# Ternarizing the next weight slices ahead of a chunk's recurrence chain instead of behind it, with the slices' loads cut in four

## The reference, cut to what matters

```python
# xn: 2048 x 1024 per sequence, x_q: xn rounded to 8 bits per row
# W_q: weights rounded to -1, 0, 1 by the mean of |W|
dt = clip(softplus(bitlinear(xn, W_dt, b_dt)), 0.001, 1.0)
x_proj = bitlinear(xn, W_x, b_x)              # 2048 columns: b_t and c_t
b_t = clip(x_proj[..., :D], -5, 5)
c_t = clip(x_proj[..., D:], -5, 5)
alpha = exp(clip(dt * A, -10, 0))
prefix = cumprod(alpha)                       # along the 2048 positions
h = prefix * cumsum(dt * b_t / prefix_shift)
s = nan_to_num(h * tanh(c_t))
x = x + s * silu(xn @ W_ternary.T)
```

## Time and profile before

| quantity | value |
|---|---|
| time, median of 2 runs | 2427.0 us (2418.78 to 2435.22) |
| the profiled execution's own time | 2431.09 us |
| its span, slowest core (core 7) | 2429.5 us |
| spans of the 8 cores | 2399.9 to 2429.5 us |
| DVE busy over the span | 1376.0 us (57%) |
| PE busy over the span | 1017.7 us (42%) |
| ACT busy over the span | 694.0 us (29%) |

### The profile page before, as it was taken

The page is one execution under the profiler, slowest core; times in us unless marked ns, Lnnn a source line. Parts: engine busy times, 40 slices in busy tenths (PEclk is TensorE's granted clock), DMA queues, the critical chain, the costliest instruction groups (busy, mean ns, idle before and its releaser), DMA issues.

```text
span 2429.5 us, 17568 instructions; the slowest of 8 cores (2399.9 to 2429.5 us)
## 1 busy us (share of the span) xinstructions
PE 1017.7 (42%) x3686; PEld 373.7 (15%) x3686; DVE 1376.0 (57%) x1730; ACT 694.0 (29%) x877; POOL 27.8 (1%) x52
## 2 busy tenths in 40 slices
PE   0321142227999999970010310413362352352351
PEld 0000000002333333320000000201120120121120
DVE  1135566654443444432222377477878878878877
ACT  0543320026555555421108300000131131131130
POOL 0000000000000000000000000000000000000000
PEclk9999999558988999985555755555785686686685
DMA  2867500013232333202223000000011011011000
GB/s 41 240 175 226 171 1 0 0 45 124 83 104 70 104 105 100 100 19 86 85 95 123 1 0 0 26 0 3 6 52 45 7 52 52 0 52 52 0 35 35
DMA packets 63375, 153.18 MB, mean 63 GB/s; under 512 B 18003, under 2 KB 18132, under 8 KB 61205
## 3 DMA queue, kind: packets, MB, share of 16 engines
q1 hardware_dynamic: 58406, 126.89, 17.4%
q0 software_dynamic: 4864, 25.17, 2.7%
HBM read 135.25 MB, written 16.78 MB: 63 GB/s over the span
## 4 chain that ended last, share of the span: by engine, by line
DVE 35%; PE 28%; DMA 11%; ACT 10%; issue 8%; DVEq 5%; ACTq 1%; SPq 0%; PEldq 0%; PEld 0%; POOLq 0%; POOL 0%
PE psB L784 9%; PE psA L767 8%; PE psA L1017 5%; DMA x1spill<-poolf 5%; DVE poolf L374 4%; DVEq L110 4%; DMA poolf<-w2t 3%; ACT poolb L584 2%; ACT poolf L556 2%; ACT poolb L512 2%; DVE poolf L673 2%; PE psB L1091 2%; DMA poolf<-w1t 2%; ACT poolf L559 2%; ACT poolb L776 1%
## 5 line engine op out<-in xcount | busy, mean ns | idle before, releaser
L784 PE MATMUL psB<-poolb 128*128 128x512 bf16 x1024 | 265.1, 396 | 37.1 <-ACTq L110 29.5
L797 DVE TENSOR_TENSOR poolb<-psB,poolb 128x512 bf16<-128x512 f32 x224 | 155.0, 692 | 199.8 <-PE psB L784 199.2
L767 PE MATMUL psA<-poolb 128*128 128x512 bf16 x1024 | 244.7, 399 | 12.9 <-DVEq L110 12.9
L1091 PE MATMUL psB<-poolb 128*128 128x512 bf16 x256 | 75.0, 459 | 405.3 <-ACTq L110 405.3
L556 ACT ACTIVATE poolf<-poolf 128x512 f32<-128x512 f32 (+1 forms) x160 | 143.8, 898 | 318.8 <-DVEq L110 257.4
L562 DVE TENSOR_SCALAR poolb<-poolf 128x512 bf16<-128x512 f32 (+1 forms) x160 | 76.9, 481 | 140.6 <-ACTq L110 125.6
L623 PE MATMUL psC<-poolf 1*128 1x512 f32 x32 | 29.8, 1027 | 295.8 <-DVEq L110 244.3
L1017 PE MATMUL psA<-poolb 128*128 128x512 bf16 x512 | 131.8, 404 | 22.5 <-DVEq L110 22.5
L559 ACT ACTIVATE poolf<-poolf 128x512 f32<-128x512 f32 (+1 forms) x160 | 129.1, 807 | 25.9 <-ACTq L110 25.9
L512 ACT ACTIVATE poolb<-poolf 128x1024 bf16<-128x1024 f32 x96 | 101.4, 1056 | 121.2 <-DMA poolf<-w2t 48.3
L1098 ACT ACTIVATE poolf<-psB,poolf 128x512 f32<-128x512 f32 x32 | 22.0, 688 | 366.4 <-DVEq L110 329.3
(11 more groups left out here) (188 smaller groups left out, 1542.8 us busy)
## 6 DMA issues: line engine op xcount, KB each, us to landing
poolf<-w2t SPq DMA_DIRECT2D x64, 512.0 KB, 4.0
poolf<-xT SPq DMA_DIRECT2D x96, 256.0 KB, 4.5
poolf<-w1t SPq DMA_DIRECT2D x32, 512.0 KB
poolf<-w1t SPq DMA_DIRECT2D x64, 256.0 KB, 3.3
poolf<-wxt SPq DMA_DIRECT2D x32, 512.0 KB, 4.2
poolf<-wdtt SPq DMA_DIRECT2D x16, 512.0 KB, 4.4
poolf<-wft SPq DMA_DIRECT2D x16, 512.0 KB, 4.1
x1spill<-poolf POOLq DMA_DIRECT2D x32, 256.0 KB, 3.6
```

The costliest lines, as they stand in the source:

```text
L767: pop_(lambda e, j=j, c=c, g=g, w1q8=w1q8: e.matmul(psA_t[:, j * 512:(j + 1) * 512], w1q8.ap(c * 512 + j * 128, c * 512 + (j + 1) * 128), ...
L784: pop_(lambda e, c=c, j=j, pbk=pbk, w2q8=w2q8, h8=h8: e.matmul(psB_t[:, pbk:pbk + 512], w2q8.ap(j * 1024 + c * 128, j * 1024 + (c + 1) * 128),
L797: vop(lambda e, pbk=pbk, oa=oa: e.tensor_add(oa.ap(), psB_t[:, pbk:pbk + 512], oa.ap()), [kB(pbk, pbk + 512), oa.key()], [oa.key()])
L1091: pop_(lambda e, c=c, g=g, dc2=dc2, pbk=pbk: e.matmul(psB_t[:, pbk:pbk + 512], wfq.ap(dc2 * 1024 + c * 128, dc2 * 1024 + (c + 1) * 128), x ...
```

## The change

Two things are changed. The load of a W_x slice is issued as four DMAs of 256 columns each instead of one of 1024, with its own key each, so that they are spread over all four load semaphores. And in the main loop, ternarizing for chunk c + 1 is recorded right behind `l1_mm(c)` and ahead of `l1_chain(c)`. The loads for chunk 1 are recorded before the loop, and those for chunk c + 2 behind the ternarizing that empties the staging buffer.

```diff
         def wx_dma(oc, par):
             stg = wstage.sub(par * 1024, 1024)
-            dma_in(stg.ap(), wxt[oc * 128:(oc + 1) * 128, :], stg.key())
+            for q in range(4):
+                dma_in(stg.ap(q * 256, (q + 1) * 256),
+                       wxt[oc * 128:(oc + 1) * 128, q * 256:(q + 1) * 256],
+                       stg.key(q * 256, (q + 1) * 256))
...
         wx_tern(0, 0)
         wx_tern(8, 1)
+        wx_dma(1, 0)
+        wx_dma(9, 1)
         for c in range(DC):
-            if c + 1 < DC:
-                wx_dma(c + 1, 0)
-                wx_dma(c + 9, 1)
             l1_mm(c)
-            l1_chain(c)
             if c + 1 < DC:
                 wx_tern(c + 1, 0)
                 wx_tern(c + 9, 1)
+                if c + 2 < DC:
+                    wx_dma(c + 2, 0)
+                    wx_dma(c + 10, 1)
+            l1_chain(c)
```

## The result

The changed kernel takes 2470.4 us in the median of 11 runs, against 2420.9 us in 10 runs of the kernel before taken beside it. The changed kernel is 1.92% slower by its ratio, with a 95% interval from 1.0155 to 1.0230. The interval lies wholly on the slower side of no change, and on both sides of the 2% line. The forecast was 2473 us, in a range of 2459 to 2490. It was worked out on a base of 2427.0 us, 6 us above the one measured now; as a difference it was +46.0 us, where the medians give +49.5 and the ratio, applied to 2420.9 us, gives +46.5.

The account below looks back on a forecast made before the run. The prediction took DVE to bound the layer 1 loop, with its idle time between chains. A cost of 80.8 us less a gain of 34.8 gave +46.0 on 2427.0, so 2473 us, in a range of 2459 to 2490.

Parts of the forecast that it names:

- What bounds the loop: Layer 1 chunk loop: goes at DVE's pace, busy 72.9 of 90.2 us; what counts is where DVE stands idle.
- The gain: Head of chunks 1 to 7: PE's standstill and most of its slow clock go, 4.97 us each, 34.8 us saved.
- The cost: Ahead of the chains of chunks 0 to 6: softplus stands behind a blocked L556, 80.8 us added in all.
- The table load: Between Abs and Exp on ACT: 1.44 us by the trace; the skill page's figure would add 7 us over six chunks.
- PE keeps its slow stretch: Rival, PE's eight groups: only the standstill is gained, the slow clock comes elsewhere; +58.3, 2485 us; 11%.
- gets 0.81 of its clock: Rival, W_dt and W_x groups: a group takes 2.65 us, gain shrinks to 6.8 in all; +74.0, 2501 us; 7%.
- The loads: W_x slice loads cut in four: hide or save nothing, 0 to 4.2 us once.
- the slack of four groups: Chunk's head: a first L1030 late behind a store does no harm; PE needs that psA quarter four groups (8.6 us) later.
- The sum: Whole kernel: 80.8 - 34.8 = +46.0 us, giving 2473.0 us, 1.9% slower.

Follow-up runs that it names:

- The two experiments: Changed kernel with softplus recorded ahead of the next chunk's ternarizing, ratio 1.0005; changed kernel ternarizing inside the staging buffer instead of shared scratch tiles, ratio 0.9942.
- the interleaved version: Ternarizing in place, two alternating slice buffers, ACT's part ahead of l1_mm(c), next chunk's four L562 among the chunk's own groups; 2383.9 us, ratio 0.9879 against the kernel before.

## Why the prediction was right, step by step

**What bounds the loop.** DVE's busy time did not move (72.92 to 72.93 us a chunk), as the first step had it. The 6.8 us by which a chunk grew are idle time of DVE; the one wait that is new, L1049's for ACT, is 7.04 us.

**The gain.** Forecast 4.97 us in each of seven chunks, measured 34.1 in all. The changed kernel's boundary is 21.48 us from E to the chain's start in chunk 7, where nothing is added: the value of the working. Both parts of it showed: the standstill is gone, and the eight groups run at 1.00. The sum came out 0.7 lower than 34.8: 0.4 because chunk 2's slot is at 21.67 where I had set all at 21.29, and the rest is chunk 1's issue of 0.54, which I had counted in this term.

**The cost.** Forecast 11.72 us in six chunks and 10.43 in chunk 0. Measured from the slot, less the 0.19 of issue that was there before, it is 11.79 in four chunks, 12.15 and 12.07 in chunks 1 and 6, and 10.46 in chunk 0. Chunk 1's excess of 0.36 is the issue of 0.54 that it had before as well, now ahead of its first L562; chunk 6's is the one late L556. Abs starts 4.35 us after the first L562 (forecast 4.26), L1049 waits 7.04 (forecast 7.0), and chunk 7 pays nothing. The two experiments that take away one of the two conditions each, the urgent work behind the blocked piece or the block, both remove the loss.

**The table load.** Abs ends at 1926.58 and Exp starts at 1928.01. These are 1.43 us on the path, now that it is exposed, as in rows 3. The 2.66 us that the Trainium skill gives ("ScalarE: Activation LUTs", What ACT_TABLE_LOAD costs) would by the prediction's estimate have made the six chunks 7 us longer, which the trace does not show; the load itself, 1.28 us, agrees.

**The clock.** The rivals in which PE keeps its slow stretch or gets 0.81 of its clock did not come: 26 us at 1.00. The second of them rested on less than the prediction says. It set the 0.81 of the earlier trace rows beside matmuls that run on all eight cores at once, but that row is of core 7 alone. PE is busy for over 73 of each 80 us on all eight cores there, and only cores 6 and 7 have the 0.81. Here is core 7, then core 5 of the same die, in the same window:

```profile
640.00:720.00 80.00, 79.18 (x296) 0.81 0.25 83
```

```profile
640.00:720.00 80.00, 75.33 (x332) 1.00 0.32 109
```

The six other cores, and all cores of the seven other traces, have 0.98 to 1.00 from 640 to 720 and from 720 to 800 us. What put two cores of a die at 0.81 is open.

**The loads.** They were to cost nothing, 0 to 4.2 us once. No L1030 waits for the store in the changed kernel, and only two L556 are released by a load, both in chunk 0 and 0.27 us behind their predecessors, where later chunks have 0.21. In the version with softplus first one L1030 did wait 3.4 us for that store, and every boundary of that kernel still is 21.3 to 21.7 us long: the slack of four groups that the forecast named is real. What I missed is the 0.11 us a chunk by which the cut loads delay L556, since that piece now lies on the path, 0.8 us in all.

**The sum.** +46.0 us is what the loop of the slowest cores shows to the decimal, and that is partly luck. The cost came out 0.8 us higher than forecast and the gain 0.7 lower; the chains, which the prediction left as they are, came out 1.4 shorter. The 1.4 us lie in DVE's wait for the chunk's Silu, 9.8 us in all before (L1104) and 8.4 after (L1107). On core 0 the chains are not shorter (512.8 and 513.2 us), and its loop grows by 47.8 us. The mechanism and the sizes of both large terms were right; the agreement beyond 2 us was not earned.

## What to carry to other kernels

An engine's program is a queue, so moving work within it moves everything that is recorded behind it. Before putting early work ahead of a chain, ask of each moved operation what it waits for at the new place, and what urgent work then stands behind it. Background work may be moved to the front only if it never waits for the engine that the urgent work serves: give it a scratch of its own, or let it stand behind the urgent operation. The place for small operations of a bounding engine is in waits that it has anyway, here 0.84 us per group behind PE.

## What the runs showed of the hardware that I had not expected

**PE's clock comes back early or late, in a pattern that goes with the chunk's length.** Behind the 50 to 63 us in which PE stands idle in each chain, it restarts with the second 16 gate matmuls at a granted clock of 0.50, and DVE waits for the Silu behind them. In the kernel before, the 16 matmuls take 6.33 us in one chunk, with 0.50 over the first 5 us, and 4.90 in the next, with 0.50 over the first 2:

```profile
1865.30 6.33 PE L1091 MATMUL psB<-poolb 128*128 128x512 bf16 x16 [50.90 <-ACTq L110]
...
1956.94 4.90 PE L1091 MATMUL psB<-poolb 128*128 128x512 bf16 x16 [51.18 <-ACTq L110]
```

and the chain alternates with them between about 64.6 and 63.5 us. In the changed kernel, with chunks of about 97 us, the two values alternate too. In the interleaved version, with chunks of 85.3 us, the 16 take 5.50 to 5.55 us in every chunk. In the version that ternarizes in place the chunks are 88.3 to 88.7 us, and the chain drifts the slow way, from 64.25 us in chunk 0 up to 64.78 in chunk 6. One of its chunks, and its DVE waits:

```profile
1946.83 6.26 PE L1094 MATMUL psB<-poolb 128*128 128x512 bf16 x16 [53.01 <-ACTq L110]
```

```profile
DVE poolf L1107 <- ACTq L110: 13.5, 8, 1.9
```

The wait is 13.5 us in all where the kernel before has 9.8, the changed kernel 8.4 and the interleaved version 7.8. Against the kernel before that is 3.7 us lost with no instruction added, about a fifth of the 17 us that the edit was to gain. That the chunk's length decides it is not shown: no run varied the length by itself.

**An ACT operation that waits on more semaphores starts a little later, though all have long been met.** The L556 of the fourth piece starts 0.27 us after its predecessor with loads in four, and 0.16 with loads in one, in kernels that are otherwise the same. That the number of semaphores is the cause is my reading; it is the one difference for this L556, since the loads have landed long before. It is nothing while it is hidden, and seven times 0.11 us once it is exposed.
